# Second attention of a transformer stack: work order of all engines, unread products, early weight loads, and who makes the second normed rows

## The reference

```
h      = h + w0 * answer0 + w1 * answer1          # best two experts of layer 0, row by row
x      = layernorm(h)                             # "first normed rows"
q,k,v  = x Wq, x Wk, x Wv   (12 heads of 16), each rounded to steps s and clipped to -4..3
a      = q k^T / (4 * 192), kept positive, rounded to steps s_attn, clipped to 7
o      = (a v), rounded to steps s_after, clipped to -4..3
h      = h + o Wproj + bproj
x2     = layernorm(h)                             # "second normed rows"
h      = h + x2 ;  logits = x2 Wr                 # router scores of 16 experts
```

## Time and profile before

| | us |
|---|---|
| median of 3 runs | 2648.91 |
| lowest, highest | 2645.78, 2661.94 |
| the profiled execution | 2652.59 |
| its span, first to last instruction | 2650.5 |
| attention1 in it, about | 597 to 861 |
| attention2 begins | 1233 |

### The profile page before, as it was taken

The page is one execution under the profiler, slowest core; times in us unless marked ns, Lnnn a source line. Parts: engine busy times, 40 slices in busy tenths (PEclk is TensorE's granted clock), DMA queues, the critical chain, the costliest instruction groups (busy, mean ns, idle before and its releaser), DMA issues. The chain is left out here.

```text
span 2650.5 us, 51944 instructions
## 1 busy us (share of the span) xinstructions
PE 2341.4 (88%) x17821; PEld 2043.9 (77%) x17821; DVE 1336.1 (50%) x3877; ACT 849.8 (32%) x2090; POOL 494.2 (19%) x583
## 2 busy tenths in 40 slices
PE   8968999987998499997999766999978899999997
PEld 8958999975776389986788655787747788888886
DVE  2663333324786711112788753555576356372744
ACT  2411222213554033332322212434344243343431
POOL 1223222321232334443122101000021000010100
PEclk8979999995787699998999856999989999999999
DMA  3124364502110276682000001000002542616355
GB/s 109 31 62 140 126 188 126 183 27 58 33 27 19 86 237 212 215 255 69 18 19 9 1 0 28 8 9 7 10 10 56 142 124 79 190 55 180 87 152 156
DMA packets 234528, 234.75 MB, mean 89 GB/s; under 512 B 29736, under 2 KB 214942, under 8 KB 234270
## 3 DMA queue, kind: packets, MB, share of 16 engines
q1 hardware_dynamic: 221822, 205.09, 27.2%
q0 software_dynamic: 11520, 27.54, 3.1%
q10 hardware_dynamic: 1056, 0.46, 0.1%
HBM read 277.77 MB, written 35.45 MB: 118 GB/s over the span
## 5 line engine op out<-in xcount | busy, mean ns | idle before, releaser
L731 PE MATMUL f_pg<-f_vxT,f_w 128*128 128x128 f32 x2112 | 259.2, 277 | 3.0 <-DVE f_vxT L801 3.0
L731 PEld LDWEIGHTS f_pg<-f_vxT,f_w 128*128 128x128 f32 x2112 | 254.5, 194 | 4.4 <-DVE f_vxT L801 4.4
L743 PE MATMUL f_po<-f_wd,f_hid 128*128 128x192 f32 x1440 | 254.3, 326 | 1.2 <-DVE f_vout L827 0.7
L743 PEld LDWEIGHTS f_po<-f_wd,f_hid 128*128 128x128 f32 x1440 | 231.2, 190 | 2.0 <-issue 1.7
L704 POOL DMA_INDIRECT f_answers<-f_vout,f_to_row x120 | 118.5, 987 | 416.4 <-DVE f_vout L825 250.2
L812 DVE TENSOR_TENSOR f_hid<-f_silu,f_pg 128x128 f32<-128x128 f32 x336 | 81.6, 284 | 206.9 <-ACT f_silu L780 192.0
L780 ACT ACTIVATE f_silu<-f_pg 128x128 f32<-128x128 f32 x336 | 78.1, 276 | 292.4 <-PE f_pg L737 272.5
L785 ACT ACTIVATE f_hid<-f_pg,f_b 128x128 f32<-128x128 f32 x384 | 106.0, 375 | 190.3 <-PE f_pg L737 190.3
L737 PE MATMUL f_pg<-f_vxT,f_wr 64*128 64x128 f32 x2112 | 150.9, 284 | 0.0
L1891 DVE TENSOR_REDUCE a_low<-a_s_bank 96x6 f32<-96x1152 f32 x64 | 86.7, 1354 | 115.8 <-PE a_s_bank L1746 115.4
L2721 PE MATMUL s_bank<-s_w,s_arena 128*128 128x192 f32 x768 | 135.0, 333 | 5.9 <-DMA s_b<-s_b_of 5.9
(11 more groups left out here) (394 smaller groups left out, 4805.9 us busy)
## 6 DMA issues: line engine op xcount, KB each, us to landing
f_wd<-in_L_ffn_W SPq DMA_DIRECT2D x64, 576.0 KB
f_wd<-in_L_ffn_WdT SPq DMA_DIRECT2D x56, 576.0 KB
f_w<-in_L_ffn_W SPq DMA_DIRECT2D x64, 384.0 KB
f_w<-in_L_ffn_WgT SPq DMA_DIRECT2D x56, 384.0 KB
f_w<-in_L_ffn_WuT SPq DMA_DIRECT2D x56, 384.0 KB
s_w<-in_w SPq DMA_DIRECT2D x64, 288.0 KB, 3.5
f_wr<-in_L_ffn_W SPq DMA_DIRECT2D x128, 96.0 KB
s_w<-in_w SPq DMA_DIRECT2D x64, 192.0 KB, 4.1
```

What stands on the lines that cost most here:

```text
L731: pe.matmul(pg[j][:, a * ROWS:(a + 1) * ROWS], lift[a][r][:, j * 128:j * 128 + 128], xT[r][:, 0, :], start=(a == 0), stop=False, skip_grou ...
L743: last = pe.matmul(po[:, 0:D], hid[r][:, j, :], wd[r][:, j, :], start=(at == 0), stop=(at == FC - 1))
```

## The change

- The order of the parts in each iteration is written anew on PE, ACT and DVE. PE had scores 0, weigh(n-1, 1), scores 1, turn_in, scores 2, queries, project_out, scores 3, weigh(n, 0), keys, scores 4, turn_normed, values, scores 5, route_scores(n-2). It now has scores 0, turn_in, scores 1, route_scores(n-3), queries, weigh(n-1, 1), scores 2 and 3, keys, project_out, scores 4 and 5, values, weigh(n, 0), turn_normed(n-2).
- `fill(count)` issues products of the identity with itself into b_bank that nobody reads: 20 and 12 before the first rows, 3 and 6 between the first products, and 3 or 6 in the first iterations in place of parts that don't exist yet.
- The second normed rows are made by ACT: DVE makes -mean times root (`shift_of`), ACT's `norm_out` multiplies and adds. It stands one iteration after DVE's norm_out of before.
- The weights of attention1 and attention2 get objects of their own that live through the experts stage; their transfers are issued on ACT's queue in tokens_of_places of the layer before. The constants of DVE are worked out before the first answers.

The core of the diff:

```diff
+        def begin(self, act):           # SecondWeights: 17 transfers, ThirdWeights: 7
+        act.dma_start(self.padded[:], halves(wqk_src)).then_inc(self.loaded, 16)
...
         @block.scalar                   # tokens_of_places
         def _(act):
+            begin_early(act)
             act.wait_ge(used, PAIRS_OF)
...
         # attention1, PE
+            def fill(count):
+                for _ in range(count):
+                    pe.matmul(b_bank[:, 0:128], k.ident[:], k.ident[:], start=True, stop=True)
+            fill(20)
+            pe.wait_ge(S["collected"], 1)
+            fill(12)
             pe.wait_ge(S["packed"], 4)
             turn_in(0)
+            fill(3)
             queries(0)
             keys(0)
             values(0)
+            fill(6)
+            for n in range(B + 3):
+                front, ahead, back = n < B, n + 1 < B, 1 <= n <= B
+                if front:
+                    scores(n, 0)
+                if ahead:
+                    turn_in(n + 1)
+                if front:
+                    scores(n, 1)
+                if n >= 3:
+                    route_scores(n - 3)
+                elif front:
+                    fill(3)
+                if ahead:
+                    queries(n + 1)
+                if back:
+                    weigh(n - 1, 1)
+                if front:
                     scores(n, 2)
+                    scores(n, 3)
+                if ahead:
+                    keys(n + 1)
+                if back:
+                    project_out(n - 1)
+                elif front:
+                    fill(6)
+                if front:
+                    scores(n, 4)
+                    scores(n, 5)
+                if ahead:
+                    values(n + 1)
+                if front:
+                    weigh(n, 0)
+                if 2 <= n <= B + 1:
                     turn_normed(n - 2)
...
         # attention1, ACT
+            def norm_out(n):
+                act.wait_ge(S["shift"], n + 1)
+                if n >= KEPT:
+                    act.wait_ge(kept[n % KEPT], 32 * (n // KEPT))
+                    act.wait_ge(S["grown"], n - KEPT + 1)
+                for t in range(2):
+                    last = nc.scalar.activation(rows2[n % KEPT][:, t, :], h[:, 2 * n + t, :], ACT.Identity,
+                                                scale=root[1][:, t, :], bias=shift[n % 2][:, t, :])
+                last.then_inc(S["rows2"], 1)
...
         # ACT per iteration: keep_scores 0, xT, keep_scores 1, keep_q, keep_o, keep_scores 2, 3, keep_k,
         #                    norm_out(n-2), keep_scores 4, 5, keep_v, x2T
...
         # attention1, DVE, per iteration
                 if front:
                     take_scores(n, 0)
+                if n >= 3:
+                    keep_logits(n - 3)
                 if second:
                     collect_part(n + 2, 0)
                 if front:
                     take_scores(n, 1)
                 if second:
                     collect_part(n + 2, 1)
+                if ahead:
+                    take_q(n + 1)
+                if back:
+                    take_o(n - 1)
                 if front:
                     take_scores(n, 2)
                     take_scores(n, 3)
+                if second:
+                    spread_in(n + 2)
                 if ahead:
                     take_k(n + 1)
                 if back:
+                    add(n - 1)
+                if front:
+                    take_scores(n, 4)
+                if back:
                     dve.wait_ge(S["added"], n)
                     spread_of(1, n - 1)
+                if second:
+                    norm_in(n + 2)
                 if front:
                     take_scores(n, 5)
+                if ahead:
+                    take_v(n + 1)
                 if back:
+                    shift_of(n - 1)
```

More of the change, by code:

```diff
@@ L536, in _, with tokens_of_places @@
             send_rows(k, pool, sent, visits, place_of)
-def tokens_of_places(k, name, place_of, from_row, to_row, slots, begin):
+def tokens_of_places(k, name, place_of, from_row, to_row, slots, begin, begin_early):
     nc = k.nc
@@ L881, in begin, with moe @@
                              ).then_inc(self.biased, 16)
-def moe(k, name, E, score, w_in1, w_in2, w_down, b1, b2, after):
+def moe(k, name, E, score, w_in1, w_in2, w_down, b1, b2, early, after):
     ROWS = 128
@@ L1211, in attention1 @@
         mv, var, root = ([one(f"{x}{r}", [H2, 2, n]) for r in range(2)] for x, n in (("mv", 2), ("var", 1), ("root", 1)))
-        half = one("half", [H2, 2, 1])
+        half, shift = one("half", [H2, 2, 1]), ring(2, "shift", [H2, 2, 1])
         p_bank, o_bank, t_bank, b_bank = (k.ps(f"a1_{x}_bank", [128, 512], ctx) for x in ("p", "o", "t", "b"))
@@ L1215, in attention1 @@
         S = {x: k.sem(f"a1_{x}") for x in (
-            "loaded", "preset", "packed", "consts", "step", "collected", "var0", "var1", "root0", "root1", "rows", "biased", "turned",
+            "shift", "preset", "packed", "consts", "step", "collected", "var0", "var1", "root0", "root1", "rows", "biased", "turned",
             "xT", "q_in", "q8", "q", "k_in", "k8", "k", "v_in", "v8", "v", "scores", "at8", "at", "weighed", "o8", "o",
@@ L1248, in store @@
                 sp.dma_start(to[:, :, D:WIDE], rows2[n % KEPT][:, :, 128:D]).then_inc(kept[n % KEPT], 16)
[L1250 to L1258, removed]
+            for m in range(6):
+                bring(m)
             for n in range(B + 1):
@@ L1540, in norm_in, with shift_of @@
                 norm_of(0, n, rows[n % 2], "rows")
[L1542 to L1546, removed]
+            def shift_of(n):
+                dve.wait_ge(S["root1"], n + 1)
+                nc.vector.scalar_tensor_tensor(out=shift[n % 2][:], in0=mv[1][:, :, 0:1], scalar=-1.0, in1=root[1][:],
+                                               op0=ALU.mult, op1=ALU.mult).then_inc(S["shift"], 1)
             def take_q(n):
@@ L1605, in _ @@
             take_v(0)
-            for n in range(B + 2):
+            for n in range(B + 3):
                 front, ahead, second, back = n < B, n + 1 < B, n + 2 < B, 1 <= n <= B
@@ L1992, in bring @@
                                  ).then_inc(got_in[m % AHEAD], 16)
-            bring(0)
-            sp.dma_start(w[:], halves(wqkv_src)).then_inc(S["loaded"], 16)
-            for m in range(1, AHEAD):
-                bring(m)
-            sp.dma_start(feat[:], feat_src).then_inc(S["loaded"], 16)
-            sp.dma_start(wp[:], halves(wproj_src)).then_inc(S["loaded"], 16)
-            for m in range(AHEAD, B):
+            for m in range(B):
                 bring(m)
```

176 lines of the change are left out of this document (79 added, 97 removed).

## The result

The kernel after takes 2681.47 us (median of 4 runs, 2675.8 to 2685.28), the kernel before 2647.35 beside it: ratio 1.0116, 95% interval 1.0081 to 1.0152. It is slower by 34 us, where I had forecast 2661 and a range of 2600 to 2686. The profiled execution took 2685.28, its span is 2683.2, 32.7 more than the span before.

What follows compares the result with a forecast made beforehand. TensorE, busy nearly throughout but often at a low clock, was taken as the bound. Loop +31.4, start -5.0, iterations 0 and 1 -11.0, third attention -3.1 gave +12.3: 2661 us against the median, range 2600 to 2686.

Steps and rivals of the forecast that it cites:

- Start of the second attention: Early weights end turn_in(0)'s load wait and unread products bring rounds in at 2.4 GHz: -5.0 us, bounds -3.8 and -8.5.
- Iterations 0 and 1: Second attention's first two iterations, at the high clock without router products, last 9.5 and 12.0 us for 32.5: -11.0.
- The loop, P = 16.5: Thirteen later iterations at 16.5 us for 14.1, mixing 14.9, 16.5 and 18.2 as quarter, half, quarter: +31.4 us.
- the case of 14.9: Loop iteration whose clock falls only at the queries' end: 14.9 us, weighted a quarter.
- norm_out on ScalarE, 0.65 the pair: In the loop, ScalarE gains two 96x192 activations, 0.65 us together, bounds 0.5 and 1.0.
- The shift, 0.2: In the loop, VectorE loses norm_out (0.66 us) and gains the shift, 0.2 us.
- Third attention, -3.1: Early weights let the third attention's turn_in start when its rows are ready: -3.1 us, bounds 0 and -3.5.
- Cost of the loads, 0: Early loads issued on ScalarE's queue in tokens_of_places, joining the first expert weights, cost 0, at worst +4 us per layer.
- Rival A: The loop's clock holds at 2.4 GHz despite the gap: 12.2 us an iteration, 2605 us in all; chance 0.26.
- Rival B: The clock falls in iteration 2 and stays low: 18.2 us an iteration, 2683 us in all; chance 0.14.
- Rival C: VectorE reaches norm_in late enough to cover the root's wait: 10.5 us an iteration, 2583 us; chance 0.10.
- The prediction's D: Fills raise nothing, rounds start at 1.2 GHz: start -3.8, iterations 0 and 1 unchanged, 2673 us; within the forecast's 0.50.

Runs made afterwards that it cites:

- the run with the roots' order: The changed kernel, but GpSimd issues root_of(0, n+2) ahead of root_of(1, n-1); ratio to the kernel before 0.9899.

## Why the prediction was right or wrong

The time lies in the range and the mechanism of the loop was the forecast's: norm_in waits for the other root, TensorE idles, the clock falls, and it comes back later in the iteration or not at all. But the point was 20 us low, the measured 1.2% lies beyond the 1% that I held likeliest (its interval, 0.8 to 1.5%, reaches below), and 4.5 us more would have left the range. By steps:

- *Start of the second attention, -5.0:* -6.6, between the bounds. The wait for the load went, and the first products ran at 2.4 GHz. That the 20 and 12 unread products end ahead of turn_in(0) was wrong: its rows are ready at 604.74 and it starts at 606.45, right behind them. The 1.7 us that this cost is nearly the 2.0 that the higher clock gives back (9.43 - 7.45, above), so they have next to no net share. Between the two profiles of the kernel before the first round moves by 2.2 us (620.46 and 622.69), so a difference of 1.6 from the forecast says little.
- *Iterations 0 and 1, -11.0:* -6.1. This step failed in part. "9.5 and 12.0, no router products" left out that the stall is there from iteration 2's turn_in on, which lies within this stretch: 2.46 us idle, the fall at 635.5, and then thin products and queries at 1.2 GHz (2.77 for 1.54). The term asked for the warm chain where the next step said that the clock is lost.
- *The loop, P = 16.5:* 16.72, +34.3 for +31.4. The stall was 1.55 us for 1.6, the idle time of TensorE 1.97 for 2.4, the clock 0.61 for "near 0.7". The three cases of the mix were not as weighed: from one weigh(n, 1) to the next seven iterations took 16.2 and five 18.0, and the last, whose second half has no next image, 14.3; the case of 14.9, a fall as late as the queries' end, did not come. Nor does TensorE idle in each iteration: behind an iteration without a rise it is late itself. The full iterations took 16.9 on average, and only with the short last one is it 16.7, so that the sum came within 3 us is in part luck.
- *norm_out on ScalarE, 0.65 the pair:* 0.97 to 0.99 (534 ns each), at the upper bound. I had taken the price from the earlier trace rows, an activation of that size that copies without scale and bias per partition; the nearest shape was not the nearest operation. Nothing hangs on it while the loop waits for the root.
- *The shift, 0.2:* mostly 0.97, and 0.15 at its shortest; it falls beside add_bias. The collision that left collect_part came to the shift. The Trainium skill (SBUF — State Buffer, "Who interferes with whom") says that a VectorE instruction with two inputs in SBUF contends with a GpSimd instruction that reads SBUF. The trace agrees: the shift, with two small inputs in SBUF, takes 0.97 beside add_bias for 0.15. This could have been seen ahead. The same section names tensor_scalar among the operations that can contend, and in the run with the roots' order the variance's tensor_scalar takes 1.00 us beside grow's 0.99 instead of 0.17.
- *Third attention, -3.1:* turn_in stands 11.8 us behind the last answers sent for 16.2, so -4.5, 1.0 beyond the bound. *Cost of the loads, 0:* likely 3, not settled; the forecast allowed up to 4 a layer.
- *Rival A (clock holds, 2605):* wrong for this kernel, right as arithmetic: with 9 products in the gap the iteration is 12.6 for its 12.2, and the ratio 0.9865 makes 2612 for its 2605. The Trainium skill (TensorE: Matmul & The Clock Gate, "Why this matters for your kernels") warns of idle gaps longer than any here; the measurements differ, since falls came behind 2.46, 1.97, 1.16 and 0.53 us in thin work, and with 4 products in the gap there was none from 610.8 to 778.0.
- *Rival B (no rise, 18.2):* five of the thirteen iterations did that, at 18.0. *Rival C (root's wait covered, P = 10.5, 2583):* not so by itself; with the order turned and the gap filled it is 11.0, and 2590 by the ratio 0.9782.
- *The prediction's D (rounds start at 1.2 GHz):* they started at 2.4 GHz, and did so without the 32 unread products too.

In the profiled executions I had +12.3 and 32.7 came. Of the 20.4 between them 14.9 lie behind the second attention (-3.1 forecast, +11.8 measured), where one kernel differs from itself by as much, so this part of the miss stays open; the rest is iterations 0 and 1 (+4.9) and the loop (+2.9), less the start (1.6) and the tail (0.8).

## What to carry to other kernels

When two operations on one in-order engine swap their neighbours, look at the queue of every engine that serves them. Here VectorE's order was turned and GpSimd's was not, and moving two lines there was worth some 42 us, 1.6%.

Where TensorE runs thin work at the high clock, look for short idle times in it. Four unread products (0.94 us) put there took another 39.6 us off, 1.5%. In the old order, where other gaps stayed open, three made the later iterations shorter and the kernel no faster.

Size such a fill by its measured price: 24 held the clock as 9 did and cost 28.5 us more at the last logits, and 2 were too few. And compare kernels that were measured beside different runs of the kernel before by their traces too, as its own median moved by 14 us here.

## What the runs showed of the hardware that was not expected

- The clock is not a matter of one gap. The same rows, idle 0.52 and 0.53 us behind 2 products, kept it in one iteration and lost it in the next; idle 0.57 us behind 9 kept it throughout. One loop with the same code had its high iterations elsewhere in two profiles (13.84 and 13.42 us). The kernel before rose at 678.7 in one profile, at 663.0 in the other, an iteration earlier: 4.6 us.
- At 1.2 GHz a loop can stay low for long: 82 us, with four whole iterations of 17.5 to 19.9 us, in the old order with three products, TensorE busy 77.66 of 80 us.
- The smallest VectorE operations lose most beside GpSimd, as a share of their time: 96x2 elements took 0.15 to 0.17 us alone and up to 1.00 beside a GpSimd operation of 96x384.
